# Merging the experts' return with the graph setup, and issuing the first stage's bulk loads from GpSimd

## The reference

```python
for g in range(G):
    iw = _topk_gate(z @ wg_inner[g], EK, E)
    moe = sum(iw[:, e:e+1] * (relu(z @ W1[g, e] + b1[g, e]) @ W2[g, e] + b2[g, e]) for e in range(E))
    out = out + gw[:, g:g+1] * _layernorm(z + moe, gln_g[g], gln_b[g])
x = x + out
# third part: h = layernorm(x) @ W, attention over the edges, each edge pair counted as often as it occurs
```

## Time and profile before

| | |
|---|---|
| median of 3 runs | 2343.44 us (2342.75 to 2345.57) |
| the profiled execution | 2332.56 us, its span 2330.8 us |
| mean granted TensorE clock | 0.92 |
| busy share of the span | PE 86%, VectorE 64%, ScalarE 49%, GpSimd 34% |
| first stage ends, ScalarE's last SiLU | 105.6 us |
| experts' return, first GpSimd work to VectorE's last | 1184.7 to 1274.8 us |
| graph setup, first work to the attention's first product | 1279.8 to 1333.1 us |

### The profile page before, as it was taken

One profiled execution on the slowest core, in us unless ns is written; L12 is line 12 of the kernel. 1 busy time (PEld: TensorE's weight loads), 2 busy tenths in 40 slices (PEclk: granted clock), 3 DMA queues, 4 the chain that ended last, 5 costly groups with the idle time before them and its releaser, 6 DMA issues. The chain is left out here.

```text
span 2330.8 us, 36639 instructions
## 1 busy us (share of the span) xinstructions
PE 1995.9 (86%) x11260; PEld 1284.6 (55%) x11261; DVE 1480.5 (64%) x2465; ACT 1132.7 (49%) x2288; POOL 794.3 (34%) x630
## 2 busy tenths in 40 slices
PE   5899999999996829999975597999999999980997
PEld 2444444444444727777732444777344777540997
DVE  1299999999995874333348675777373777438011
ACT  5777777777773314555510514665002666210332
POOL 4188888888880012444453000000000000001453
PEclk9999999999998957999988698999999999995998
DMA  5565565555552424778544313000012100331894
GB/s 162 168 164 154 153 155 156 155 155 154 155 155 80 93 82 147 264 254 261 186 127 125 103 44 116 22 22 1 18 44 89 57 22 1 109 110 35 227 275 93
DMA packets 200742, 285.13 MB, mean 122 GB/s; under 512 B 116698, under 2 KB 128677, under 8 KB 196543
## 3 DMA queue, kind: packets, MB, share of 16 engines
q0 software_dynamic: 98272, 142.08, 22.0%
q1 hardware_dynamic: 100158, 137.67, 19.4%
q10 hardware_dynamic: 2209, 4.07, 0.5%
HBM read 233.52 MB, written 49.84 MB: 122 GB/s over the span
## 5 line engine op out<-in xcount | busy, mean ns | idle before, releaser
L565 POOL DMA_INDIRECT p_s<-node_table,e_src_rows x320 | 497.9, 1556 | 106.9 <-issue 106.9
L2007 PE MATMUL g_psO<-g_h,g_ring 125*125 125x257 f32 x1600 | 372.7, 388 | 20.0 <-DVE g_ring L2139 10.6
L2007 PEld LDWEIGHTS g_psO<-g_h,g_ring 125*125 125x125 f32 x1600 | 296.8, 190 | 92.4 <-DVE g_stage L2133 26.6
L703 PE MATMUL p_psW<-e_w,p_hid 64*125 64x512 f32 x640 | 274.6, 652 | 39.6 <-ACT z L580 25.3
L622 DVE TENSOR_TENSOR g_b<-z,p_s 125x1536 f32<-125x1536 f32 x160 | 273.1, 1746 | 0.0
L711 PE MATMUL p_psM<-g_b 125*32 125x384 f32 x648 | 244.9, 525 | 15.3 <-DVE g_b L622 6.5
L580 ACT ACTIVATE z<-p_psW 125x512 f32<-125x512 f32 x320 | 186.7, 583 | 132.3 <-PE p_psW L703 132.3
L715 PE MATMUL p_psM<-g_b 125*32 125x256 f32 x648 | 216.3, 418 | 0.0
L714 PE MATMUL p_psM<-g_b 125*32 125x256 f32 x648 | 207.6, 404 | 0.0
L713 PE MATMUL p_psM<-g_b 125*32 125x256 f32 x648 | 190.8, 421 | 0.0
L585 ACT ACTIVATE p_of<-e_node_ids,z 125x314 bf16<-125x314 f16 x320 | 176.0, 550 | 9.2 <-PE p_psC L720 5.9
(11 more groups left out here) (357 smaller groups left out, 3756.8 us busy)
## 6 DMA issues: line engine op xcount, KB each, us to landing
p_ring<-in_L_ffn_weights SPq DMA_DIRECT2D x32, 1025.0 KB, 7.2
slot_rows<-p_y POOLq DMA_DIRECT2D x70, 256.0 KB, 4.4
p_w1s<-in_L_ffn_w SPq DMA_DIRECT2D x16, 1024.0 KB, 8.9
g_a<-in_L_ffn_w SPq DMA_DIRECT2D x16, 1024.0 KB, 7.0
hidden<-g_b SPq DMA_DIRECT2D x40, 250.0 KB, 3.3
p_hid<-hidden SPq DMA_DIRECT2D x160, 62.5 KB
g_rb<-receiver_rows SPq DMA_DIRECT2D x16, 610.4 KB
p_s<-node_table,e_src_rows POOLq DMA_INDIRECT x320, 5.1
```

The lines of the kernel that those rows point to most:

```text
L565: pool.indirect_dma_start(s[:, g % 4, c, :, :].rearrange("p k u -> p (k u)"), None, node_table, bass.IndirectOffsetOnAxis(ap=src_rows[:, g ...
L703: nc.tensor.matmul(psW[c % 2][0:P, :], hid[part, b, c // 2, :], w4[part, :], start=True, stop=True)\
L2007: last = nc.tensor.matmul(psO[0:P, j, 0:HW], ring[:, i % RING, j * P:(j + 1) * P], h[:, s, hd, :], start=s == 0, stop=s == T - 1)
```

## The change

`combine` takes the place of the experts' third block and of `graph_setup`. Per tile, VectorE now does mix(t+1), finish(t) with the statistics of the new row of x at its end, difference(t+2) for the counts, in tiles 4 to 7 a fourth of the attention vectors, and norm(t). TensorE turns counts and normed rows between the products; the products of the next tile (`offsets(t + 2)`) stand ahead of the turning of the normed rows and of the counts. The accumulators of the offsets (`psB`) and of the sum (`psF`) have one buffer each instead of two, and the counts are turned through two banks (`psC`) instead of six, in three parts that each wait for the copy of the part two before. `wide_t` is cleared by VectorE. `wide`, `chosen_gate`, `slots` and `small` move to `spare`, a region that outlives the experts' stage; `small` is cleared and loaded in the experts' second block, after the first gathers there. The semaphores' clean-up of the experts' stage, which came after the return, now comes before it.

In `prepare` the 13 bulk loads move from the start of ScalarE's list to GpSimd's, behind a wait for the first round's features and ahead of the two large clears.

```diff
@@ prepare, GpSimd's list
                                allow_small_or_imprecise_dtypes=True).then_inc(ids, 1)
+                pool.wait_ge(ea_in[0], 64)
+                rows = x.rearrange("(t p) d -> p t d", p=P)
+                for k in range(T // 2):
+                    pool.dma_start(xs[:, 2 * k:2 * k + 2, :], rows[:, 2 * k:2 * k + 2, :]).then_inc(x_in[k], 16)
+                pool.dma_start(dsts[:], dst.rearrange("(g e) -> g e", e=EG)).then_inc(dst_in, 16)
+                pool.dma_start(wu[:, 0, :], w_up0).then_inc(up_in, 16)
...
                 nc.gpsimd.memset(tables.macc[:], 0.0).then_inc(ids, 1)
                 nc.gpsimd.memset(tables.cacc[:], 0.0).then_inc(ids, 1)
@@ prepare, ScalarE's list
-                for k in range(T // 2):
-                    act.dma_start(xs[:, 2 * k:2 * k + 2, :], rows[:, 2 * k:2 * k + 2, :]).then_inc(x_in[k], 16)
-                act.dma_start(dsts[:], dst.rearrange("(g e) -> g e", e=EG)).then_inc(dst_in, 16)
...
@@ routed_experts, first block
-                    nc.gpsimd.memset(small[:], 0.0).then_inc(zeros, 1)
-                    pool.wait_ge(zeros, 1)
@@ combine, TensorE
+                def offsets(t):
+                    pe.wait_ge(wide_ok, t * TOP // 4 + 1)
+                    if t:
+                        pe.wait_ge(moe_ok, t)
+                    ...
+                def turn_counts(t):
+                    pe.wait_ge(looped, t + 1)
+                    for k, (a, b) in enumerate(PARTS):
+                        n = NPARTS * t + k
+                        if n >= 2:
+                            pe.wait_ge(cnt_ok, n - 1)
+                        ...
+                for t in range(T):
+                    if t + 2 < T:
+                        offsets(t + 2)
+                    if t:
+                        turn_rows(t - 1)
+                    if t + 1 < T:
+                        gains(t + 1)
+                        sums(t + 1)
+                    if t + 2 < T:
+                        turn_counts(t + 2)
+                turn_rows(T - 1)
@@ combine, VectorE
+                difference(0)
+                difference(1)
+                mix(0)
                 for t in range(T):
+                    if t + 1 < T:
+                        mix(t + 1)
+                    finish(t)
+                    if t + 2 < T:
+                        difference(t + 2)
+                    if 4 <= t < 4 + KD:
+                        v.wait_ge(att_in, 32)
+                        v.wait_ge(ws_in[t - 4], 16)
+                        attention_vectors(nc, v, wa_ok, ws, att, prod, wa, t - 4)
+                    norm(t)
```

More of the change, by code:

```diff
@@ L1060 @@
 J = TOP * TOP
+WIDE = X + 2 * NG
 BLOCKS = (N * J + X * 127) // 128
@@ L1068, with for_combine, routed_experts @@
 SLOTS = BLOCKS * 128
-def routed_experts(nc, queue, lg, z, weights, b2, gln_g, gln_b, z_rows, slot_rows, out, spare, x_new):
+def for_combine(spare):
+    at = X * X + 2 * J * T * X + T * (NG + 1) * NE
+    sizes = [T * TOP * WIDE, J * T, J * T]
+    parts = []
+    for size in sizes:
+        parts.append(spare[0:P, at:at + size])
+        at += size
+    return (parts[0].rearrange("p (t a m) -> p t a m", t=T, a=TOP), parts[1].rearrange("p (j t) -> p j t", j=J),
+            parts[2].bitcast(I32).rearrange("p (j t) -> p j t", j=J),
+            spare[:, 0:3 * D].rearrange("p (k d) -> p k d", k=3))
+def routed_experts(nc, queue, lg, z, weights, b2, gln_g, gln_b, z_rows, slot_rows, out, spare):
     H = 256
@@ L1408, in _ @@
                         gather(b)
+                    nc.gpsimd.memset(small, 0.0).then_inc(zeros, 1)
                     for b in range(BLOCKS):
@@ L1696, with combine @@
 TH = T // 2
-def graph_setup(nc, xs, counts, xt, cnt, far, w, ws, att_src, att_dst, wa):
+def combine(nc, queue, spare, xs, slot_rows, x_new, counts, xt, cnt, far, w, ws, att_src, att_dst, wa):
     ctx = ExitStack()
@@ L1712, in graph_setup @@
         away = sb("away", [P, 1])
-        rows16 = sb("rows16", [P, 2, NW], U16)
+        wide_t = sb("wide_t", [128, T * TOP, P])
+        yg = sb("yg", [P, YB, J, D])
+        moe = sb("moe", [P, 2, TOP, D])
+        stats = sb("stats", [P, 2, TOP, 6])
+        mv = sb("mv", [P, 2, TOP, 2])
+        std = sb("std", [P, 2, TOP])
+        rstd = sb("rstd", [P, 2, TOP])
+        row_stats = sb("row_stats", [P, T, 6])
+        row_mv = sb("row_mv", [P, T, 2])
+        row_std = sb("row_std", [P, T])
+        row_rstd = sb("row_rstd", [P, T])
+        normed = sb("normed", [P, 2, D])
+        rows16 = sb("rows16", [P, RB, NW], U16)
         rows = sb("rows", [P, 2, 4 * CQ])
@@ L1752, in _ @@
                 tick(nc.gpsimd.memset(away[:], -FAR))
+                for t in range(T):
+                    if t >= YB:
+                        pool.wait_ge(moe_ok, t - YB + 1)
+                    for j in range(J):
+                        pool.indirect_dma_start(yg[:, t % YB, j, :], None, slot_rows,
+                                                bass.IndirectOffsetOnAxis(ap=slots[:, j, t:t + 1], axis=0))\
+                            .then_inc(back[t % YB], 16)
+            @block.tensor
@@ L1754, in _ @@
             @block.vector
             def _(v):
[L1756 to L1767 removed]
+                tick = Ticks(v, sem("mixed"))
@@ new lines, in finish @@
+                def finish(t):
+                    s = t % 2
+                    v.wait_ge(gain_mm, t + 1)
+                    v.wait_ge(mv_ok, t + 1)
+                    for a in range(TOP):
+                        last = nc.vector.scalar_tensor_tensor(moe[:, s, a, :], moe[:, s, a, :], mv[:, s, a, 0:1],
+                                                              psG[0:P, a, :], ALU.subtract, ALU.mult)
+                    last.then_inc(scaled, 1)
+                    v.wait_ge(std_ok, t + 1)
+                    r = tick(nc.vector.reciprocal(rstd[:, s, :], std[:, s, :]))
+                    tick.wait(r)
+                    v.wait_ge(scaled, t + 1)
+                    v.wait_ge(sum_mm, t + 1)
+                    m = tick(nc.vector.scalar_tensor_tensor(xs[:, t, :], moe[:, s, 0, :], rstd[:, s, 0:1],
+                                                            psF[0:P, :], ALU.mult, ALU.add))
+                    tick.wait(m)
+                    nc.vector.scalar_tensor_tensor(xs[:, t, :], moe[:, s, 1, :], rstd[:, s, 1:2], xs[:, t, :],
+                                                   ALU.mult, ALU.add).then_inc(out_ok, 1)
+                    v.wait_ge(out_ok, t + 1)
+                    n = tick(nc.vector.bn_stats(row_stats[:, t, :], xs[:, t, :]))
+                    tick.wait(n)
+                    nc.vector.bn_aggr(row_mv[:, t, :], row_stats[:, t, :]).then_inc(row_mv_ok, 1)
@@ new lines, in norm @@
+                def norm(t):
+                    v.wait_ge(row_std_ok, t + 1)
+                    n = tick(nc.vector.reciprocal(row_rstd[:, t:t + 1], row_std[:, t:t + 1]))
+                    if t >= 2:
+                        v.wait_ge(x_turned, t - 1)
+                    tick.wait(n)
+                    nc.vector.tensor_scalar(normed[:, t % 2, :], xs[:, t, :], row_mv[:, t, 0:1], row_rstd[:, t:t + 1],
+                                            ALU.subtract, ALU.mult).then_inc(x_ok, 1)
```

420 lines of the change are left out of this document (186 added, 234 removed).

## The result

The changed kernel takes **2326.14 us** (median of 4 runs, 2324.69 to 2326.57) against 2343.1 us (2338.84 to 2345.57): ratio 0.9929, interval 0.9915 to 0.9944, or 17.0 us less. The forecast was 2315, in the range 2305 to 2330: the time lies inside, but 10.9 us above the forecast. The difference from before is under 2%, and clear of the spread. The profiled execution took 2326.57 us, its own median; the one of before had lain 10.9 us under its median, so the two traces are compared stage by stage and not by their spans.

A forecast was written before the change was run, and what follows sets the result against it. VectorE was taken to bound the experts' return, with no engine full in the counts' part and ScalarE held by load issue at the start. Gains of 15.5 + 12.7 = 28.2 us from 2343.4 gave 2315, range 2305 to 2330.

The forecast's parts named there:

- The merged stage: Experts' return and counts' setup in one block: the attention's first product comes 15.5 us earlier, at 1317.6 instead of 1333.05.
- VectorE is the bound: Merged stage: VectorE sets the pace throughout, a steady tile of 10.6 us, 13.4 with attention vectors.
- First mix: Start of the merged stage: first mix at 1199.3, 10.46 + 1.7 us behind the first gather at 1187.1.
- charge for held-up issues: Start of the merged stage: VectorE's work beside the gathers holds up GpSimd's issues, 1.2 us charged once.
- VectorE's sum: Merged stage: VectorE's work on ten tiles, differences, attention vectors and waits adds up to 116.1 us.
- Clean-up: Ahead of the merged stage: semaphore clean-up costs 1.5 us (between 0 and 5.1), about what moving the clear gives back.
- TensorE's clock: Merged stage: TensorE idles little enough to get the higher clock, near 1.0, needing 8.1 us of a 10.6 us tile.
- The first stage: Start of the program: earlier first SiLU gives 14.9 us, less 2.2 us waiting for x, a gain of 12.7 us.
- Loads bound round 4: Rival, first stage: x lands slowly beside the stores, so the stage gives 6 us; 2322 us, chance 0.12.
- GpSimd's queue: Rival, first stage: GpSimd is held by its issues as ScalarE was, the stage gives 4.4 us; 2323.5 us, chance 0.12.
- a loose one: Rival, merged stage: each tile loses 1 us waiting between TensorE, ScalarE and VectorE, 10 us; 2325 us, chance 0.14.
- TensorE at the lower clock as the bound of a tile: Rival, merged stage: TensorE needs 13.6 us, making 16.2 us a tile and the kernel slower; 2361 us, chance 0.05.

The follow-up runs named there:

- the doubled statistics: Changed kernel with VectorE taking the statistics of each finished row twice in all ten tiles; 2323.72 us, ratio 0.9951 to the kernel before.
- the run without interleaving: Changed kernel's single block, but each engine does all mixing and finishing first, then all counts and norms; 2334.20 us, ratio 0.9992 to the kernel before.
- that part alone: Kernel before with only the thirteen bulk loads moved from ScalarE to GpSimd; 2341.14 us, ratio 0.9986 to the kernel before.
- The two repairs: Changed kernel with GpSimd's load issues spread between its clears and two buffers for each of hidden's four tiles; together 2305.24 us, ratio 0.9874 to before.

## Why the prediction was right, and where it was not

**The merged stage: right, term by term.** Forecast 15.5 us. In the two traces the stretch from the last store of `slot_rows` to the attention's first product went from 154.1 to 138.8: 15.3; over all executions the seam went from 173.3 to 157.5: 15.9. That the sum is so close is in part luck: the first mix came 1.2 us earlier behind the first gather than forecast, VectorE's work took 1.9 us more, and the first gather came 0.6 us earlier behind the last store.
- *VectorE is the bound.* Shown by the doubled statistics (5.6 of 6.9 us) and by 5.1 us of named waits in 117. Tile 10.4 us (forecast 10.6); with attention vectors the mixes stand 13.15 apart (forecast 13.4).
- *First mix.* Forecast 10.46 + 1.7 behind the first gather; it was 10.9. The charge for held-up issues was right in kind and too large: the first tile's four issues took 5.2 us where they had taken 4.9, and the next four 5.4 (more on this below).
- *VectorE's sum.* Forecast 116.1 us from the first mix to the last norm; it was 118.0. Two waits for gathered rows (2.2 and 0.6 us, where 1.4 was charged) and one of 1.3 for `p_psF` are more than the difference; the steady tile gave 0.2 us back each time.
- *Clean-up.* Costed at 1.5, given back by the clear. The pair came out at 0.6 us to the good (8.17 to 7.59 us from last store to first gather).
- *TensorE's clock.* I expected near 1.0; it was 0.90 and 0.81. TensorE had the room, so that cost at most the waits above.

**Which issues are held up.** The prediction charged 1.2 us for a gather's issue beside VectorE's work. In these rows the start of an issue lies inside a difference:

```profile
1197.71 1.46 DVE L1789 TENSOR_TENSOR p_rows<-p_rows 125x1252 f32<-125x1252 uint16 x1 [2.05 <-DMA p_rows<-counts]
1198.81 1.46 POOL L1648 DMA_INDIRECT p_yg<-slot_rows,g_b  x1 [0.31 <-issue]
...
1201.26 1.46 DVE L1789 TENSOR_TENSOR p_rows<-p_rows 125x1252 f32<-125x1252 uint16 x1 [1.76 <-DMA p_rows<-counts]
1202.08 1.73 POOL L1648 DMA_INDIRECT p_yg<-slot_rows,g_b  x1 [0.31 <-issue]
```

Of the stage's 40 issues, the seven that started while a VectorE instruction with two inputs in SBUF ran (L1789, L1806) took 1.29 to 1.87 us, each about 1.21 us plus what was left of that instruction, less 0.1. The other 33 took 1.21 to 1.28. The 2.48 us of the earlier trace rows fit: of the first of L622's two instructions (3.42 us for both) some 1.4 us were left when the issue began. So an issue loses at most the rest of one instruction. The Trainium skill (SBUF — State Buffer, Who interferes with whom) has a VectorE instruction with two SBUF inputs contend with a GpSimd instruction that reads SBUF, and infers that writing descriptors is spared. That the charge would be nothing does not hold in the trace: an issue that starts inside such an instruction is held up. A gather takes its row numbers from SBUF, so its start may count as such a read; no run here tests that.

What the prediction did not say, and the run without interleaving showed: putting both stages into one block gains nothing by itself. The pause between the blocks (5.1 us) goes, but longer waits and tile-by-tile statistics take as much; the 16.6 us by which the seams differ (174.0 and 157.5) come from laying the counts' part, which no engine filled, beside the return, which VectorE filled. What a single block with batches of ten and without the longer wait would give was not run.

**The first stage: the step failed.** The prediction took 12.7 us, "14.9 - 2.2": everything that the earlier first SiLU gives, less a wait for x. The 14.9 itself stands there without a source, between the 13.9 and the 15.6 that the text works out for the first SiLU; that came 15.5 us earlier, so this is not where it failed. Measured: 0.6 us in the first trace, 2.1 as a mean, 3.3 in the timing of that part alone (interval 1.2 to 5.4). x was not late: the aggregation of its statistics ran at 31.07, where the sum had its end at 40.1, so the 2.2 us for it were not there either. What failed was an item that the sum did not hold. It asked when the moved loads would arrive, and when GpSimd would be free (its clears were done at 44.1, forecast 50.0), but not what the loads would do to transfers that were already there. The stores of `hidden` keep their place in the program, and each of their four buffers is free only once its store has landed; with the DMA engines full they took up to 14.4 us, ScalarE stood for 8.6 us, TensorE behind it, and TensorE then ran its next rounds at the lower clock. The two repairs show it: with the loads paced and the buffers doubled ScalarE comes to its root at 37.94 us, where the prediction had 37.9 ahead of its charge for x, and the gathers start 12.1 us earlier than in the first profile. How the loss divides between the waits and the lower clock behind them was not separated.

**The rivals.** "Loads bound round 4" (2322) was nearest in its mechanism, by another path: the loads bound the rounds ahead of it, through the stores. GpSimd's queue did not fill: the five pieces of x took 6.1 us to issue and the eight others 4.4. The tile packed, although the number given for a loose one (2325) is the one closest to the 2326 measured; that is chance. TensorE at the lower clock as the bound of a tile did not occur.

**The experts' first block**, costed at nothing, gave nothing: VectorE waits 1.97 us for GpSimd's constants where it had waited 1.96, and the two comparisons are put together 13.3 us behind the start of the first in both traces (830.0 and 843.3, now 836.3 and 849.6).

**The sum.** 2343.4 - 28.2 was 10.9 us too low, and the term of the first stage (12.7 against 1 to 3) accounts for it. The time came to lie inside the range because the range had been drawn over the first three rivals, not because the sum held.

## What to carry to other kernels

When a load is moved earlier, cost what it does to the transfers already in flight there, and ask which engine waits for one of those to land before it can write again; the gain came near the forecast only when those buffers were doubled and the loads spread out. When two stages are merged, look for one that fills an engine and one that fills none: here the gain came from laying one beside the other, and one block with the two still in sequence gave nothing. And before two traces are compared by their spans, see how long a stage takes that the change does not touch.

## What the runs showed of the hardware

- With thirteen bulk loads in flight the 16 DMA engines showed a share of 1.06 and 338 GB/s for 6 us, and the stores of 250 KB on another queue landed after up to 14.4 us instead of 6.9 (their median stayed at 3.3).
- While ScalarE waited, TensorE was busy for 2.77 of the 6 us from 24 to 30, and its clock then was 0.50 and 0.51 from 30 to 42; where the wait was gone, the clock stayed at 1.00 up to 36 us and was 0.50 from 42 to 48, behind ScalarE's root (busy for 3.07 of the 6 us before). But in the kernel before TensorE had no work from 18 to 24 us, 2.31 us of it from 24 to 30, and a clock of 1.00 from there to 54. So a gap ahead of it was not enough by itself.
- The edges' stage, with the same instructions, took 720 to 733 us: 729.8 to 732.8 in one set of runs, 720.0 to 724.8 in the two others, and 720.1 and 727.0 in the first profiles of before and after.
- A gather's issue on GpSimd took 1.21 to 1.28 us, and 1.29 to 1.87 when it started inside a VectorE instruction with two inputs in SBUF (seven of 40). In the kernel before, 1.20 to 1.28 and, for eight of 40, 1.42 to 1.74.
- The norm (L1851, one input in SBUF) took 0.88 us in the two tiles in which a gather's issue was under way when it began, and 0.55 in the eight others.
